# Root columns moved into PSUM and rotation tables moved to GpSimd, in a fused attention and feed-forward kernel on one core

## The chip, the cores and the metric

The kernel runs on one core of a Trainium2 chip. The metric is the time of one execution on the device, in microseconds (us). Engines are named as in the profile: PE is the matrix engine, PEld its weight load, DVE the vector engine, ACT the scalar engine, POOL GpSimd, SP the engine whose queue issues the DMAs. SBUF is the large on-chip buffer, PSUM the smaller one into which PE writes.

## The reference

Everything is float32. A linear attention with its norms comes first, then six layers of the loop below, then a last norm; the change touches the loop alone.

```python
for i in range(6):                       # x is (2, 1024, 128)
    x = attn_layer(shift_tokens(x), Wqkv[i], q_scale[i], k_scale[i], Wo[i]) + x
    x = ffn_layer(shift_tokens(x), ln_g[i], ln_b[i], W1[i], b1[i], W2[i], b2[i]) + x

def attn_layer(x, Wqkv, qs, ksc, Wo):    # 16 heads of 64
    q, k, v = split(x @ Wqkv)
    q = l2norm(q) * qs;  k = l2norm(k) * ksc
    q = q * cos * scale + rotate_half(q) * sin * scale
    k = k * cos / scale + rotate_half(k) * sin / scale
    out = local_attention(q, k, v)       # windows of 32, softmax over 64 keys
    return out @ Wo

def ffn_layer(x, g, bln, W1, b1, W2, b2):
    xn = (x - mean) / sqrt(var + 1e-05) * g + bln
    a, gate = split(xn @ W1 + b1)        # 341 each
    return a * gelu(gate) @ W2 + b2
```

## The kernel before

The 2 x 1024 tokens are 16 blocks of 128. Six layers make 96 blocks, and one step of the main loop works on a pair of them: 48 pairs, `m` = 0 to 47. The loop is software-pipelined. In step `m` the engines project, square and rotate pair `m`, do scores and softmax of pair `m-1`, finish attention, output projection and the centring of the feed-forward norm of pair `m-2`, spread the norm of pair `m-3`, and do the feed-forward matmuls of pair `m-4`. Six steps are unrolled ahead of a loop in registers, four more drain it. Each engine has its own order of instructions, written out by hand in its `step(m)`, and engines meet only by semaphores (`S[...]`, each waited on for a count).

What matters for the change:

- **The rotation tables.** `tables(n, u)` (DVE, L1276) multiplies the rotary table of block `n` (cos, sin for q, cos, sin for k: 4 x 64 columns) by the layer's learned scales into `table[:, u]`, once for each block, at the head of the DVE's step. `turn_cos` (L1287) and `turn_sin` (L1298, two halves) multiply a projection in PSUM by them. POOL adds the two products (`add_q`, `add_k`, L1456).
- **The roots.** `norm_square` (L1304) leaves the sums of squares of 16 heads for q and k of both blocks in `ss` (64 columns). `find_roots(m)`, near the end of the DVE's step, turns them and two columns of variance of the feed-forward norm of pair `m-2` into 67 inverse square roots: L1313 and L1318 write `minus_half`, L1326 forms a first guess on the bits, and three Newton rounds of L1330, L1333 and L1336 follow, each instruction waiting for the one before. All of `minus_half`, `root_t` and `root` are in SBUF.
- **Who waits for the roots.** POOL's `scale_q`, `scale_k` (L1484) multiply the rotated q and k by them: one at the end of its step `m`, three at the head of step `m+1`. PE's `turn_q` and `turn_k` (L786) transpose those. DVE's `residual2(m-4)` (L1386) comes behind `find_roots(m)` in the DVE's order; it raises `x_ready`, for which PE's first `ff_up` (L871) of the next step waits. `ff_down` (L879), the last thing in PE's step, needs a count of `refined` that L1313 and L1318 give.
- **POOL's step** in order: `scale_k`, `scale_q`, `fold_q` (L1469), `scale_k`, `add_q`, `fold_k`, `take_max` (L1495), `add_k`, `take_max`, `fold_q`, `weigh`, `weigh` (L1500), `fold_k`, `add_q`, `add_k`, `scale_q`. The first `weigh` is awaited by PE's `turn_probs(2m-2)` (L786, from `probs`).
- **PE's step** from its middle: both projections at L781, `out_project` (L839) into `pm_out`, projection of k, `turn_probs`, `spread_rstd` (L860), `ff_center` (L846) into `pm_out`, projection of v (which waits for `q_turned`, so for L1298), `ff_var` (L852), `attend` (L830), `ff_down` (L879); then, in the next step, `turn_probs`, projection of q (L781), `ff_up` (L871), `turn_q`, projection of k, `turn_k`, `ff_up` into `pm_out`, and so on.
- **PSUM** is full: `r0`, `r1`, `r2` and `pm`, each two banks. `pm_norm` and `pm_out` are the two banks of `pm`.

Of the kernel before, what the change touches and what calls it, by code (L numbers as in the profile page):

```python
# [19 lines left out]
P = 128  # L20
# [34 lines left out]
def bcast(ap, axis, count):  # L55

    wide = ap.unsqueeze(axis)
    shape = list(wide.shape)
    shape[axis] = count
    return wide.broadcast_to(shape)  # L60
# [566 lines left out]
def layers(nc, weights, xT, ident, mean_w, center_w, eps):  # L627

    with ExitStack() as ctx:
        def sb(name, shape):  # L630
            return ctx.enter_context(nc.sbuf_tensor(name, shape, F32))
# [8 lines left out]
        window, rope, scales = weights.window, weights.rope, weights.scales  # L640


        table = sb("table", [P, 2, 4, DH])
        xs1 = sb("xs1", [P, 2, P])
        squares = sb("squares", [P, 2, INNER])
        ss = sb("ss", [P, QK_ROOTS + 1])
        minus_half = sb("minus_half", [P, ROOTS])
        root_t = sb("root_t", [P, ROOTS])
        root = sb("root", [P, ROOTS])
        warm = sb("warm", [P, 1])  # L650
        warm_exp = sb("warm_exp", [P, 1])
# [21 lines left out]
        hid = sb("hid", [P, 3, W2])  # L673
        r0, r1, r2, pm = psum("r0"), psum("r1"), psum("r2"), psum("pm")
        pm_norm, pm_out = pm[:, 0:512], pm[:, 512:1024]

        names = (
            "v_spread0 v_spread1 "
# [25 lines left out]

            return isinstance(n, int) and n == 0

        def run(eng, step):

            for m in range(FILLED):
                step(m)  # L710
            with eng.Fori(FILLED, PAIRS) as m:
                step(m)
            for m in range(PAIRS, PAIRS + BEHIND):
                step(m)

        def pair_at(m):
# [57 lines left out]
        def _(pe):  # L774
# [108 lines left out]
            def step(m):  # L883
# [78 lines left out]
                if runs(m - 4):  # L962
                    if runs(m - 3):
                        pe.wait_ge(S["xc_squared"], m - 2)
                    elif runs(m - 3):
                        pe.wait_ge(S["residual1"], m - 2)
                    elif runs(m - 5):
                        pe.wait_ge(S["gated"], 3 * (m - 5) + 2)
                    else:
                        pe.wait_ge(S["xc_squared"], m - 3)  # L970
                    ff_up(m - 4, 1, pm_out)
                if runs(m - 1):
                    if runs(m):
# [48 lines left out]
                if runs(m - 2):  # L1022
                    if runs(m - 4):
                        pe.wait_ge(S["gated"], 3 * (m - 4) + 2)
                    elif runs(m - 3):
                        pe.wait_ge(S["xc_squared"], m - 2)
                    elif runs(m - 3):
                        pe.wait_ge(S["residual1"], m - 2)
                    elif runs(m - 5):
                        pe.wait_ge(S["gated"], 3 * (m - 5) + 2)  # L1030
                    elif runs(m - 4):
                        pe.wait_ge(S["xc_squared"], m - 3)
                    elif runs(m - 4):
                        pe.wait_ge(S["residual1"], m - 3)
                    out_project(m - 2)
                if runs(m):
                    if runs(m - 1):
# [233 lines left out]

        @block.vector
        def _(dve):
            def tables(n, u):

                dve.tensor_tensor(table[:, u, :, :].rearrange("p k d -> p (k d)"),  # L1276
                                  rope[:, bass.ds(n % BPB, 1), :, :].rearrange("p a k d -> p (a k d)"),
                                  scales[:, bass.ds(n // NB, 1), :, :].rearrange("p a k d -> p (a k d)"),
                                  ALU.mult).then_inc(S["tabled"], 1)

            def turn_cos(n, u, k, src, squared, turned, transposed):

                dve.wait_ge(S["tabled"], n + 1)
                dve.wait_ge(S[squared], n + 1)
                if not isinstance(n, int) or n >= 2:
                    dve.wait_ge(S[transposed], n - 1)
                dve.tensor_tensor(rot[:, u, k, :, :, :].rearrange("p h a d -> p h (a d)"),  # L1287
                                  src[:, :].rearrange("p (h d) -> p h d", h=HEADS),
                                  bcast(table[:, u, 2 * k, :], 1, HEADS), ALU.mult).then_inc(S[turned], 1)

            def turn_sin(n, u, k, src, turned, added):

                if not first(n):
                    dve.wait_ge(S[added], n)
                v = src[:, :].rearrange("p (h a d) -> p h a d", h=HEADS, a=2)
                for a in range(2):
                    sin = table[:, u, 2 * k + 1, 32 * a:32 * a + 32]
                    dve.tensor_tensor(rot_sin[:, k, :, a, :], v[:, :, 1 - a, :], bcast(sin, 1, HEADS),  # L1298
                                      ALU.mult).then_inc(S[turned], 1)

# [6 lines left out]
            def find_roots(m):  # L1307

                before = ROOT_OPS * m
                if runs(m):  # L1310
                    dve.wait_ge(S["q_summed"], 2 * (m + 1))
                    dve.wait_ge(S["k_summed"], 2 * (m + 1))
                    dve.tensor_scalar(minus_half[:, 0:QK_ROOTS + 1], ss[:, :],  # L1313
                                      1e-24, -0.5, ALU.max, ALU.mult)\
                       .then_inc(S["refined"], 1 if runs(m - LAG) else 2)
                if runs(m - LAG):
                    dve.wait_ge(S["var_done"], m - LAG + 1)
                    dve.tensor_scalar(minus_half[:, QK_ROOTS + 1:ROOTS], pm_norm[:, 0:2], 1e-5, -0.5, ALU.add, ALU.mult)\  # L1318
                       .then_inc(S["refined"], 1 if runs(m) else 2)
                dve.wait_ge(S["refined"], before + 2)  # L1320
                if runs(m - 1):
                    dve.wait_ge(S["q_scaled"], 2 * m)
                    dve.wait_ge(S["k_scaled"], 2 * m)
                if runs(m - LAG - 1):
                    dve.wait_ge(S["rstd_spread"], m - LAG)
                dve.tensor_scalar(root[:, :].bitcast(I32), minus_half[:, :].bitcast(I32), -0.5, GUESS,  # L1326
                                  ALU.mult, ALU.add).then_inc(S["refined"], 1)
                for i in range(NEWTON):
                    dve.wait_ge(S["refined"], before + 3 + 3 * i)
                    dve.tensor_tensor(root_t[:, :], minus_half[:, :], root[:, :], ALU.mult)\  # L1330
                       .then_inc(S["refined"], 1)
                    dve.wait_ge(S["refined"], before + 4 + 3 * i)
                    dve.tensor_tensor(root_t[:, :], root_t[:, :], root[:, :], ALU.mult)\  # L1333
                       .then_inc(S["refined"], 1)
                    dve.wait_ge(S["refined"], before + 5 + 3 * i)
                    dve.scalar_tensor_tensor(out=root[:, :], in0=root_t[:, :], scalar=1.5, in1=root[:, :],  # L1336
                                             op0=ALU.add, op1=ALU.mult).then_inc(S["refined"], 1)
# [52 lines left out]

            def step(m):
                if runs(m):
                    tables(2 * m, 0)
                    tables(2 * m + 1, 1)
                    turn_cos(2 * m, 0, 0, r0, "q_squared", "q_turned", "qT_done")
                    turn_sin(2 * m, 0, 0, r0, "q_turned", "q_added")
                if runs(m - 4):
# [48 lines left out]
        def _(pool):  # L1446
# [46 lines left out]
            def take_max(n, u):  # L1493
                pool.wait_ge(S["maxed"], n + 1)
                pool.tensor_tensor(sm[:, u, :, :], sm[:, u, :, :], bcast(rowmax[:, :], 2, 2 * WIN), ALU.subtract)\  # L1495
                    .then_inc(S["max_taken"], 1)

            def weigh(n, u):
                pool.wait_ge(S["inverted"], n + 1)
                pool.tensor_tensor(probs[:, u, :, :], probs[:, u, :, :], bcast(rinv[:, u, :], 2, 2 * WIN), ALU.mult)\  # L1500
                    .then_inc(S["weighted"], 1)

            def step(m):
                if runs(m - 1):
                    scale_k(2 * m - 2, 0)
                    scale_q(2 * m - 1, 1)
                if runs(m):
                    fold_q(2 * m, 0)
                if runs(m - 1):
                    scale_k(2 * m - 1, 1)  # L1510
                if runs(m):
                    add_q(2 * m, 0)
                    fold_k(2 * m, 0)
                if runs(m - 1):
                    take_max(2 * m - 2, 0)
                if runs(m):
                    add_k(2 * m, 0)
                if runs(m - 1):
                    take_max(2 * m - 1, 1)
                if runs(m):  # L1520
                    fold_q(2 * m + 1, 1)
                if runs(m - 1):
                    weigh(2 * m - 2, 0)
                    weigh(2 * m - 1, 1)
                if runs(m):
                    fold_k(2 * m + 1, 1)
                    add_q(2 * m + 1, 1)
                    add_k(2 * m + 1, 1)
                    scale_q(2 * m, 0)

            run(pool, step)


def last_norm(nc, x1, xT, center_w, eps, out):
# [118 lines left out]
```

## Time and profile before

| | us |
|---|---|
| median of 3 runs | 1858.31 |
| lowest, highest | 1854.05, 1860.98 |
| the profiled execution | 1854.16 |
| its span in the trace | 1852.3 |

| engine | busy us | share of the span |
|---|---|---|
| PE | 1673.8 | 90% |
| DVE | 1562.0 | 84% |
| POOL | 1488.4 | 80% |
| ACT | 1219.1 | 66% |

The linear attention fills roughly the first 120 us; the loop runs from there to about 1838 us. Within it the pattern repeats every 34.2 us, and PE's granted clock is full from 340 us on. A line such as L1484 is a line of the code below, and several operations of one kind can share one. In a timeline row the number in square brackets is how long the engine was idle just before, with what released it.

### The profile page before, as it was taken

How to read it: one execution, taken by the hardware profiler on the slowest of the kernel's cores; microseconds unless marked ns; L12 is line 12 of the kernel's file. 1: busy time of each engine (PE TensorE's matmuls, PEld its weight loads, DVE VectorE, ACT ScalarE, POOL GpSimd, SP SyncE). 2: the span in 40 equal slices, each digit the busy share in tenths (PEclk: the TensorE clock that was granted, in tenths of full speed). 3: DMA queues.
4: the chain of work that ended last, by engine and by line, in shares of the span. 5: the costliest groups of instructions: out<-in, count | busy, mean ns of one | idle time of the engine just before them, and what ended most of it. 6: DMA issues, size and time to landing. Idle time of an engine off the chain costs nothing. (4 is left out here: it accounts for less than half of the span.)

```text
span 1852.3 us, 76505 instructions
## 1 busy us (share of the span) xinstructions
PE 1673.8 (90%) x30992; PEld 1195.4 (65%) x30992; DVE 1562.0 (84%) x2309; ACT 1219.1 (66%) x2072; POOL 1488.4 (80%) x823
## 2 busy tenths in 40 slices
PE   4957889899999999999999999999999999999985
PEld 3634566667667666676676676676666766766664
DVE  6878667898898898988989989988889989899853
ACT  3435455677777767767677777777677676777754
POOL 3568777788888888888888888888888888888851
PEclk7979889999999999999999999999999999999999
DMA  4002132121332221332212232222242223222220
GB/s 136 1 13 57 48 92 60 47 68 45 81 105 75 54 60 48 94 96 68 68 50 67 75 103 55 68 67 66 67 106 59 54 68 79 57 68 68 58 57 23
DMA packets 80697, 121.87 MB, mean 66 GB/s; under 512 B 16776, under 2 KB 29574, under 8 KB 79750
## 3 DMA queue, kind: packets, MB, share of 16 engines
q1 hardware_dynamic: 80646, 121.14, 24.9%
q8 instruction: 38, 0.62, 0.1%
q14 instruction: 13, 0.11, 0.0%
HBM read 19.36 MB, written 1.05 MB: 11 GB/s over the span
## 5 line engine op out<-in xcount | busy, mean ns | idle before, releaser
L781 PE MATMUL r<-wqkv,xs 128*128 (+1 forms) x1152 | 560.7, 618 | 13.4 <-DVE rot_sin L1298 4.3
L1484 POOL TENSOR_TENSOR rot<-rot,root 128x1024 f32<-128x1024 f32 x192 | 377.7, 1987 | 120.6 <-DVE root L1336 120.6
L1456 POOL TENSOR_TENSOR rot<-rot,rot_sin 128x1024 f32<-128x1024 f32 x192 | 451.8, 2364 | 1.6 <-DVE rot_sin L1298 1.6
L781 PEld LDWEIGHTS r<-wqkv,xs 128*128 128x128 f32 x1152 | 210.0, 195 | 213.4 <-issue 197.7
L1131 ACT ACTIVATE squares<-r 128x512 f32<-128x512 f32 x384 | 217.6, 598 | 80.5 <-PE r L781 79.3
L1287 DVE TENSOR_TENSOR rot<-r,table 128x1024 f32<-128x1024 f32 x192 | 232.8, 1213 | 21.0 <-PE r L786 9.6
L1469 POOL TENSOR_TENSOR squares<-squares 128x512 f32<-128x512 f32 x192 | 244.5, 1273 | 6.6 <-ACT squares L1131 6.5
L1500 POOL TENSOR_TENSOR probs<-probs,rinv 128x1024 f32<-128x1024 f32 x96 | 182.7, 1903 | 81.2 <-DVE rinv L1358 81.2
L1298 DVE TENSOR_TENSOR rot_sin<-r,table 128x512 f32<-128x512 f32 x384 | 242.6, 673 | 0.0
L786 PE MATMUL r<-square,rot 128*128 128x128 f32 x1536 | 208.4, 279 | 17.3 <-POOL rot L1484 11.8
L786 PEld LDWEIGHTS r<-square,rot 128*128 128x128 f32 x1536 | 169.5, 141 | 81.2 <-issue 27.5
L1495 POOL TENSOR_TENSOR sm<-sm,rowmax 128x1024 f32<-128x1024 f32 x96 | 182.6, 1902 | 45.4 <-DVE rowmax L1350 45.1
L1343 DVE TENSOR_TENSOR sm<-r,window 128x1024 f32<-128x1024 f32 x96 | 117.6, 1225 | 109.6 <-PE r L814 109.6
L1166 ACT ACTIVATE qT<-r 128x1024 f32<-128x1024 f32 x96 | 98.2, 1023 | 165.6 <-PE r L786 165.6
L871 PE MATMUL pm<-xn,w 128*128 128x256 f32 (+1 forms) x576 | 153.4, 390 | 58.4 <-DVE xT L1386 57.8
L830 PE MATMUL r<-pT,vwin 64*64 64x32 f32 x12288 | 202.9, 221 | 2.6 <-issue 2.6
L830 PEld LDWEIGHTS r<-pT,vwin 64*64 64x64 f32 x12288 | 191.7, 137 | 13.5 <-issue 12.9
L839 PE MATMUL pm<-attnT,wo 128*128 128x256 f32 x768 | 175.5, 382 | 1.2 <-issue 1.2
L839 PEld LDWEIGHTS pm<-attnT,wo 128*128 128x128 f32 x768 | 147.0, 192 | 41.2 <-issue 23.3
L1276 DVE TENSOR_TENSOR table<-rope,scales 128x256 f32 (+1 forms) x96 | 155.5, 1658 | 10.2 <-issue 10.1
L871 PEld LDWEIGHTS pm<-xn,w 128*128 128x128 f32 (+1 forms) x576 | 93.9, 180 | 107.7 <-issue 87.0
L1116 ACT ACTIVATE kT<-r 128x1024 f32<-128x1024 f32 x96 | 98.3, 1024 | 96.6 <-PE r L786 91.4
(123 smaller groups left out, 2723.2 us busy)
## 6 DMA issues: line engine op xcount, KB each, us to landing
vwin<-vtok SPq DMA_DIRECT2D x576, 128.0 KB, 2.3
vwin<-vtok SPq DMA_DIRECT2D x384, 64.0 KB, 2.0
wqkv<-in_wqkv SPq DMA_DIRECT2D x6, 1536.0 KB, 8.3
wo<-in_wo SPq DMA_DIRECT2D x6, 512.0 KB, 4.9
w<-in_w SPq DMA_DIRECT2D x6, 341.0 KB, 2.9
x<-in_x SPq DMA_DIRECT2D x4, 256.0 KB, 3.6
rope<-in_rope SPq DMA_DIRECT2D x1, 1024.0 KB
out_x<-y SPq DMA_DIRECT2D x4, 256.0 KB, 2.3
```

The lines of the kernel that those rows point to most:

```text
L781: pe.matmul(dst[:, c * 512:(c + 1) * 512], xs1[:, u, :], w.rearrange("p a n -> p (a n)"), start=True, stop=True).then_inc(S[done], 1)
L786: last = pe.transpose(dst[:, f * P:(f + 1) * P], src[:, f * P:(f + 1) * P], ident)
L830: last = pe.matmul(dst[DH * s:DH * (s + 1), at + WIN * w:at + WIN * (w + 1)], vwin[half, u, w, 2 * i + s, :], pT[half, u, (FT // 2) * s + ...
L839: last = pe.matmul(pm_out[:, 0:W2], wo[:, f, :], attnT[:, (f % 2) * (FT // 2) + f // 2, :], start=(f == 0), stop=(f == FT - 1))
L871: last = pe.matmul(dst[0:rows, half * W2:(half + 1) * W2], w1[:, half * FF + at:half * FF + at + rows], xn2[:, :], start=True, stop=True)
L1131: last = act.activation(squares[:, k, c * 512:(c + 1) * 512], src[:, c * 512:(c + 1) * 512], ACT.Square)
L1287: dve.tensor_tensor(rot[:, u, k, :, :, :].rearrange("p h a d -> p h (a d)"), src[:, :].rearrange("p (h d) -> p h d", h=HEADS), bcast(table ...
L1298: dve.tensor_tensor(rot_sin[:, k, :, a, :], v[:, :, 1 - a, :], bcast(sin, 1, HEADS), ALU.mult).then_inc(S[turned], 1)
L1456: pool.tensor_tensor(r, r, rot_sin[:, k, :, :, :].rearrange("p h a d -> p h (a d)"), ALU.add)\
L1469: pool.tensor_tensor(halves[:, :, 0, :], halves[:, :, 0, :], halves[:, :, 1, :], ALU.add)\
L1484: pool.tensor_tensor(r, r, bcast(root[:, at:at + HEADS], 2, DH), ALU.mult)\
L1500: pool.tensor_tensor(probs[:, u, :, :], probs[:, u, :, :], bcast(rinv[:, u, :], 2, 2 * WIN), ALU.mult)\
```

## The change

- `minus_half` and `root_t` are no longer SBUF tensors but the first 134 columns of `pm_out`. `root` stays in SBUF. L1313 now comes behind the wait for the variance and runs in every step, since other contents of the bank destroy its columns in between; PE waits for all of the roots of the step before ahead of `ff_up` into `pm_out` and of `out_project`.
- The tables are multiplied on POOL, one instruction for both blocks of a pair (512 columns), a step ahead, between the second `fold_q` and the first `weigh`. `table` has two buffers. DVE's `turn_cos` and `turn_sin` address theirs by a register.

```diff
-        table = sb("table", [P, 2, 4, DH])
+        table = sb("table", [P, 2, 2, 4, DH])
...
-        minus_half = sb("minus_half", [P, ROOTS])
-        root_t = sb("root_t", [P, ROOTS])
...
+        minus_half, root_t = pm_out[:, 0:ROOTS], pm_out[:, ROOTS:2 * ROOTS]
...
+                    pe.wait_ge(S["refined"], ROOT_OPS * (min(m, PAIRS + LAG) if isinstance(m, int) else m))
                     ff_up(m - 4, 1, pm_out)
...
+                    pe.wait_ge(S["refined"], ROOT_OPS * (min(m, PAIRS + LAG) if isinstance(m, int) else m))
                     out_project(m - 2)
...
-            def tables(n, u):
-
-                dve.tensor_tensor(table[:, u, :, :].rearrange("p k d -> p (k d)"),
-                                  rope[:, bass.ds(n % BPB, 1), :, :].rearrange("p a k d -> p (a k d)"),
-                                  scales[:, bass.ds(n // NB, 1), :, :].rearrange("p a k d -> p (a k d)"),
-                                  ALU.mult).then_inc(S["tabled"], 1)
-
             def turn_cos(n, u, k, src, squared, turned, transposed):
 
-                dve.wait_ge(S["tabled"], n + 1)
+                dve.wait_ge(S["tabled"], n // 2 + 1)
...
-                                  bcast(table[:, u, 2 * k, :], 1, HEADS), ALU.mult).then_inc(S[turned], 1)
+                                  bcast(table[:, bass.ds((n // 2) % 2, 1), u, 2 * k, :].rearrange("p a d -> p (a d)"),
+                                        1, HEADS), ALU.mult).then_inc(S[turned], 1)
...
-                    sin = table[:, u, 2 * k + 1, 32 * a:32 * a + 32]
+                    sin = table[:, bass.ds((n // 2) % 2, 1), u, 2 * k + 1, 32 * a:32 * a + 32]\
+                        .rearrange("p a d -> p (a d)")
...
                 if runs(m):
                     dve.wait_ge(S["q_summed"], 2 * (m + 1))
                     dve.wait_ge(S["k_summed"], 2 * (m + 1))
-                    dve.tensor_scalar(minus_half[:, 0:QK_ROOTS + 1], ss[:, :],
-                                      1e-24, -0.5, ALU.max, ALU.mult)\
-                       .then_inc(S["refined"], 1 if runs(m - LAG) else 2)
                 if runs(m - LAG):
                     dve.wait_ge(S["var_done"], m - LAG + 1)
+                dve.tensor_scalar(minus_half[:, 0:QK_ROOTS + 1], ss[:, :],
+                                  1e-24, -0.5, ALU.max, ALU.mult)\
+                   .then_inc(S["refined"], 1 if runs(m - LAG) else 2)
+                if runs(m - LAG):
                     dve.tensor_scalar(minus_half[:, QK_ROOTS + 1:ROOTS], pm_norm[:, 0:2], 1e-5, -0.5, ALU.add, ALU.mult)\
-                       .then_inc(S["refined"], 1 if runs(m) else 2)
+                       .then_inc(S["refined"], 1)
...
             def step(m):
                 if runs(m):
-                    tables(2 * m, 0)
-                    tables(2 * m + 1, 1)
...
+            def tables(m):
+
+                if not isinstance(m, int) or m >= 2:
+                    pool.wait_ge(S["q_turned"], 6 * (m - 1))
+                    pool.wait_ge(S["k_turned"], 6 * (m - 1))
+                pool.tensor_tensor(table[:, bass.ds(m % 2, 1), :, :, :].rearrange("p a u k d -> p (a u) (k d)"),
+                                   rope[:, bass.ds((m % PPB) * 2, 2), :, :].rearrange("p a k d -> p a (k d)"),
+                                   bcast(scales[:, bass.ds(m // PPL, 1), :, :].rearrange("p a k d -> p (a k d)"), 1, 2),
+                                   ALU.mult).then_inc(S["tabled"], 1)
...
                 if runs(m):
                     fold_q(2 * m + 1, 1)
+                if runs(m + 1):
+                    tables(m + 1)
                 if runs(m - 1):
                     weigh(2 * m - 2, 0)
...
-            run(pool, step)
+            pool.wait_ge(S["tables_loaded"], 7 * 16)
+            tables(0)
+            run(pool, step, PAIRS - 1)
```

## Rows read from the trace of the kernel before

**Rows 1.** The page: busy time, share of the span and instructions of each engine.
```profile
PE 1673.8 (90%) x30992; PEld 1195.4 (65%) x30992; DVE 1562.0 (84%) x2309; ACT 1219.1 (66%) x2072; POOL 1488.4 (80%) x823
```

**Rows 2.** Busy time in the steady stretch: PE, PEld, DVE, ACT, POOL, clock, DMA.
```profile
340.00:1800.00 1460.00, 1377.53 (x26812) 996.94 (x26811) 1287.04 (x1859) 1025.84 (x1692) 1253.77 (x678) 1.00 0.27 69
```

**Rows 3.** Groups of PE, same stretch: busy us, mean ns, idle before and releaser.
```profile
L871 PE MATMUL pm<-xn,w 128*128 128x256 f32 x340 | 91.5, 392 | 53.9 <-DVE xT L1386 53.9
...
L879 PE MATMUL pm<-hid,w 128*128 128x256 f32 x168 | 47.3, 404 | 12.2 <-DVE minus_half L1318 12.2
```

**Rows 4.** Timeline of PE over the end of one step and the next one's head.
```profile
1047.62 1.04 PE L786 MATMUL r<-square,probs 128*128 128x128 f32 x8
...
1048.93 0.60 PE L846 MATMUL pm<-xs,center_w 128*128 128x256 f32 x2
1049.62 1.98 PE L781 MATMUL r<-wqkv,xs 128*128 x4
1051.43 0.50 PE L852 MATMUL pm<-square,xcsq 128*128 128x1 f32 x4
1051.86 2.07 PE L830 MATMUL r<-pT,vwin 64*64 64x32 f32 x128
1054.23 1.56 PE L879 MATMUL pm<-hid,w 128*128 128x256 f32 x6 [0.30 <-DVE minus_half L1318]
...
1056.50 1.88 PE L781 MATMUL r<-wqkv,xs 128*128 x4
1059.63 1.13 PE L871 MATMUL pm<-xn,w 128*128 128x256 f32 x4 [1.25 <-DVE xT L1386]
```

**Rows 5.** Timeline of DVE, same stretch, and one row a pair earlier.
```profile
1019.83 2.21 DVE L1326 TENSOR_SCALAR root<-minus_half 128x67 int32<-128x67 int32 x1
...
1052.83 1.10 DVE L1313 TENSOR_SCALAR minus_half<-ss 128x65 f32<-128x65 f32 x1
1053.86 0.15 DVE L1318 TENSOR_SCALAR minus_half<-pm 128x2 f32<-128x2 f32 x1
1054.04 2.22 DVE L1326 TENSOR_SCALAR root<-minus_half 128x67 int32<-128x67 int32 x1
1056.29 0.23 DVE L1330 TENSOR_TENSOR root_t<-minus_half,root 128x67 f32<-128x67 f32 x1
...
1058.39 0.23 DVE L1336 SCALAR_TENSOR_TENSOR root<-root_t,root 128x67 f32<-128x67 f32 x1
1058.86 0.48 DVE L1386 SCALAR_TENSOR_TENSOR xT<-pm,cols,mid 128x256 f32 x1 [0.24 <-issue]
1059.58 3.34 DVE L1276 TENSOR_TENSOR table<-rope,scales 128x256 f32 x2 [0.24 <-issue]
```

**Rows 6.** Timeline of POOL over the same stretch.
```profile
1041.64 1.90 POOL L1495 TENSOR_TENSOR sm<-sm,rowmax 128x1024 f32<-128x1024 f32 x1
1043.50 1.28 POOL L1469 TENSOR_TENSOR squares<-squares 128x512 f32<-128x512 f32 x1
1044.74 1.90 POOL L1500 TENSOR_TENSOR probs<-probs,rinv 128x1024 f32<-128x1024 f32 x1
1048.42 1.90 POOL L1500 TENSOR_TENSOR probs<-probs,rinv 128x1024 f32<-128x1024 f32 x1 [1.78 <-DVE rinv L1358]
...
1051.51 4.69 POOL L1456 TENSOR_TENSOR rot<-rot,rot_sin 128x1024 f32<-128x1024 f32 x2
1058.70 5.99 POOL L1484 TENSOR_TENSOR rot<-rot,root 128x1024 f32<-128x1024 f32 x3 [2.50 <-DVE root L1336]
```

**Rows 7.** Three lines of DVE, each alone: duration in ns, min/median/max.
```profile
L1326 DVE TENSOR_SCALAR root<-minus_half x50: 195/2212/2287, 141.4 to 1820.5; 128x67 int32<-128x67 int32 x50
...
L1276 DVE TENSOR_TENSOR table<-rope,scales x96: 416/2015/2123, 119.8 to 1743.7; 128x256 f32 x84, 128x256 f32<-128x256 f32 x12
...
L1371 DVE TENSOR_TENSOR xhat<-xc,pm x48: 408/411/422, 249.0 to 1829.6; 128x256 f32<-128x256 f32 x48
L1371 DVEq FUSED_REGOPS  x42: 125/127/127, 366.7 to 1766.4; - x42
```

More of the change, by code:

```diff
@@ L705, in first, with run @@
             return isinstance(n, int) and n == 0
-        def run(eng, step):
+        def run(eng, step, end=PAIRS):
             for m in range(FILLED):
                 step(m)
-            with eng.Fori(FILLED, PAIRS) as m:
+            with eng.Fori(FILLED, end) as m:
                 step(m)
-            for m in range(PAIRS, PAIRS + BEHIND):
+            for m in range(end, PAIRS + BEHIND):
                 step(m)
```

## The prediction

> **What bounds the kernel now.** I read the page first: no engine is full, PE comes nearest, then DVE and POOL [rows 1]. The busy times of the steady stretch say how much room there is. L1326 comes at 1019.83 and again at 1054.04 [rows 5], so a pair takes 34.2 us, and 1460 us are 42.7 pairs. PE is idle 1460 - 1377.5 = 82.5 us there, 1.93 us in each pair, so a pair can't take less than 34.2 - 1.93 = 32.3 us by PE's work. DVE needs 30.1 us in each pair, POOL 29.4 [rows 2]. So PE is the bound but for its small idle times, and the question of every part of the change is what it does to these.
>
> The groups of PE then say whose they are: 53.9 us in front of `ff_up` behind DVE's `xT` and 12.2 us in front of `ff_down` behind DVE's `minus_half`, 66.1 of the 82.5 us [rows 3]. In the timeline of one step they are 1.25 and 0.30 us [rows 4].
>
> The DVE's timeline beside POOL's shows why `xT` is late. L1313 starts at 1052.83 and takes 1.10 us for 65 columns; L1326 starts at 1054.04 and takes 2.22 us for 67, while the Newton instructions of the same width take 0.23 [rows 5]. POOL runs two `add` from 1051.51 to 1056.20, so about 2.35 us each: the first ends near 1053.9, the second at 1056.20. L1313 ends at 1053.93, L1326 at 1056.26 [rows 5, 6]. Each ends just after a POOL instruction does. L1326 can take 195 ns and has a median of 2212; the tables' L1276 can take 416 ns and has a median of 2015 [rows 7]. These work SBUF to SBUF. L1318, which reads PSUM, starts in between and takes 0.15 us though the second `add` has begun [rows 5, 6]; L1371, one input in PSUM and one in SBUF, never takes more than 422 ns [rows 7]. I read this as: a DVE instruction that works on SBUF alone waits for the POOL instruction in progress, one with an operand in PSUM does not.
>
> **The roots' columns in PSUM.** L1313 then writes PSUM and L1326 reads it. Without the waits they cost what the Newton instructions do, 0.23 us: 1.10 + 2.22 - 0.46 = 2.86 us less for each pair [rows 5]. The last L1336 ends at 1058.62 now, so at 1055.76 then; `xT` ends at 56.48 instead of 59.34 [rows 5] (the leading 10 is left off from here). L1313's new place behind `var_done` costs nothing: `ff_var` ends at 51.93, DVE comes there at 52.83 [rows 4, 5].
>
> What follows on PE: L1318 ends near 53.2, before `attend` ends at 53.93, so `ff_down` starts at 53.93 and not at 54.23. The projection then ends at 58.08, `xT` is there since 56.48 (PE started 0.29 us after its end before, so 56.77), and `ff_up` starts at once [rows 4, 5]. Both PE stalls go, 66.1 / 42.7 = 1.55 us for each pair. What is late next is `turn_q`: POOL is free at 56.20, later than the roots, and its first `scale` takes 1.90, to 58.10 (1.90 is what L1495 takes at the same width, and what a scale takes once DVE's tables don't hold it up); PE comes there at 58.08 + 1.03 = 59.1 [rows 4, 6]. That is 1.0 us of cover. The two `pe.wait_ge` on `refined` come long after the roots and cost nothing.
>
> The trace has no DVE instruction that writes PSUM. From below, the price is nothing: L1318 takes 0.15 us for two columns, the Newton instructions 0.23 for 67, which are 0.08 apart for 65 columns more [rows 5]. From above, I take a doubled pace of the nine Newton instructions and L1326, 0.26 us each (L1330 starts at 56.29, the ninth at 58.39, 0.263 apart [rows 5]): 2.6 us more. The cover is 0.44 us (roots at 55.76, POOL free at 56.20) and 1.0 us at `turn_q`, 1.4 together, so it decides from 0.14 us for each of ten instructions; the upper end would give back 1.2 us a pair. I take the lower end, since the nearest rows read PSUM without a surcharge.
>
> The Trainium skill speaks against that: its page "VectorE: DVE Perf Modes", section on the TRN2 errata, gives 120 fixed cycles for an instruction from PSUM and 58 from SBUF. At 0.96 GHz that is 65 ns more, an estimate of 0.65 us for the ten. By it the roots would come at 56.41, POOL's scale would end 0.2 us later, and the sum would be the same. The trace doesn't bear the rule out for reads: two columns from PSUM took 146 ns in all.
>
> **The tables off DVE.** Two L1276 take 3.34 us, directly behind `xT` and ahead of `turn_cos` [rows 5]. Nobody on PE waits for `turn_cos` in that place, so this is DVE idle time gained, not path. It has one more effect: three scales take 5.99 us for 3 x 1.90, 0.29 us of POOL's time lost to the tables in between [rows 6]. DVE falls to 30.1 - 3.3 - 2.9 = 23.9 us a pair and can't bind by amount.
>
> **The tables on POOL.** A POOL instruction on 512 columns from two inputs takes 1.28 us (L1469), on 1024 columns 4.69 / 2 = 2.35 (L1456), and one whose second input repeats 1.90 for 1024 (L1500) [rows 6]. So it is (2.35 - 1.28) / 512 = 2.09 ns a column and 0.21 us fixed, and with a repeating input (1.90 - 0.21) / 1024 = 1.65 ns, which gives 1.06 us for 512. Between 1.06 and 1.28 I take 1.28, of which 1.24 show up in the pace (43.50 to 44.74). Its register arithmetic is hidden under the running `fold` as L1371's 127 ns are, or exposed with the 0.24 us of the DVE's tables [rows 5, 7]; I take half, 0.12.
>
> The place is the first `weigh`: it starts at 44.74 and then at 44.74 + 1.24 + 0.12 = 46.10, and ends at 48.00 instead of 46.64. PE starts `turn_probs` at 47.62 [rows 4, 6]. Everything ahead of it on POOL is tied to PE (`take_max` follows the scores), so this doesn't shift away: PE stalls 0.38 us. Of it 0.09 is swallowed: PE waits from 49.53 to 49.62 in front of the projection of v for DVE's `turn_sin`, which isn't delayed [rows 4]. Net 0.29 us a pair. The second `weigh` has 1.78 us of idle time ahead of it and isn't moved [rows 6]. The bounds: 1.06 and nothing exposed costs 0 (`weigh` ends at 47.7, and 0.09 is swallowed); 1.24 and 0.24 cost 0.41.
>
> The DVE's twelve turns of a pair now have register addresses. L1371's shows as 127 ns under a running instruction with no idle time of its own [rows 7]; I take nothing. If exposed, the place is the two `turn_sin` ahead of PE's projection of v, which are on PE's heels: 2 x 0.24 = 0.5 us a pair.
>
> **The sum.** The stalls go in the 44 steps that have both (m = 4 to 47): 44 x 1.55 = 68.2 us. The table's stall comes in 47: 47 x 0.29 = 13.6 us. Net -54.6. The span goes from 1852.3 to 1797.7, a profiled execution from 1854.16 to about 1799.6. The median of the runs shown is 1858.31, 4 us above the profiled one, and I expect the same of the new kernel: 1858.3 - 54.6 = 1803.7, so **1804 us**. By the bounds of the table alone it is 1790 to 1809.
>
> **The rivals.**
>
> *The forecast*, both stalls go and a small one comes, 1790 to 1815 us: 0.56. A pair takes about 32.9 us.
>
> *More given back*: Newton in PSUM is slower than 0.14 us an instruction above today's, or `turn_sin`'s addresses are exposed. The first at its upper end gives back 1.2 us x 44 = 53 us, 1857 (the chance of that far end is small); the second 0.5 x 47 = 23 us, 1827. Between them, 1815 to 1848: 0.20. For it speaks that no row shows a PSUM write; against it, L1318 and L1371.
>
> *More gained*: the table's stall is hidden, and the 0.38 us a pair of PE's idle time that is neither stall shrinks with DVE freed. At most 44 x 1.93 = 85 us, 1773; I put 1775 to 1790 at 0.12.
>
> *POOL becomes the bound.* It would have 29.4 - 0.3 + 1.3 = 30.4 us of work in a pair of 32.9. It binds by amount only if the table took over 3.8 us, three times the nearest row; part of the 0.06 at 1850 to 1867, no change.
>
> *The other side: PSUM doesn't free DVE from POOL.* Then L1313 and L1326 end with POOL's instructions as before, `xT` ends at 59.34, both stalls stay, and only the table's 0.29 us x 47 = 14 us is new: 1872. It decides only if L1326 still waits: if L1313 alone did, the roots would come 0.9 us later than forecast, at 56.6, and nearly all of the gain would stay, but if L1326 alone did, none of the 1.25. L1318 and L1371 speak against it. Chance 0.06.
>
> **The numbers.** A measurement of this kernel can tell about 0.5% (9 us) from no change. Faster 0.56 + 0.20 + 0.12 = 0.88; within 0.5%, 0.06; slower 0.06. The range 1784 to 1840 holds the forecast, half of the further gain and most of what is given back, and leaves out about 0.2.
>
> **What would show it.** In the new profile: L1313 and L1326 at 0.2 to 0.3 us; no idle time in front of L871 behind `xT` nor of L879 behind `minus_half`; POOL's scale without its 2.50 us wait for `root`; a POOL instruction of 1.05 to 1.3 us for the table; a new wait of PE's `turn_probs` for `probs` near 0.3 us; DVE idle while it waits for ACT's squares. The prediction is wrong if L1326 still takes 2 us, if the Newton pace is above 0.40 us, or if PE has a new stall above 1 us in a pair.

## The result: 0.943 of the time before, twice the gain that was forecast

The changed kernel takes 1751.18 us (median of 4 runs, 1747.19 to 1756.07) against 1856.18 for the kernel before on the same chips. The ratio is 0.9434, 95% interval 0.9394 to 0.9473: 105 us less. The forecast was 1804 us (54.6 less), with a range of 1784 to 1840. The sign was right and the mechanism did what it should, but the gain was nearly twice its size and the time lies below the range.

The page of the changed kernel, its busy times (its span is 1745.4 us):

```profile
PE 1638.7 (94%) x30992; PEld 1203.5 (69%) x30992; DVE 1279.3 (73%) x2215; ACT 1219.8 (70%) x2072; POOL 1528.9 (88%) x871
```

The busy times of its steady stretch, columns as in [rows 2]:

```profile
340.00:1700.00 1360.00, 1340.91 (x26548) 1003.05 (x26547) 1030.93 (x1779) 1023.76 (x1686) 1276.27 (x712) 1.00 0.28 74
```

A pair is measured here from one `residual1` to the next. In the kernel before, 38 of them lie between 431.9 and 1695.3 us: 1263.4 / 37 = 34.15 us. In the changed one, 41 lie between 408.4 and 1688.4: 1280 / 40 = 32.00 us. From the first of the 48 to the last it is 1612.8 us before and 1506.9 after, 105.9 of the 106.9 us by which the spans differ. So the whole gain is in the loop, 2.15 us in each pair of the steady part; 1.26 was forecast (1.55 - 0.29). The first four distances between them give more: 203.9 to 363.7 us before, 200.8 to 344.4 after, 16.2 us less and not 4 x 2.15 = 8.6. PE's granted clock isn't full there in either kernel (200 to 270 and 270 to 340 us: 0.88 and 0.95 before, 0.93 and 0.98 after), and in the kernel before it is still 0.97 from 340 to 400 us, so "full from 340 us on" was a little too early.

The DVE's timeline at the roots shows the wait for POOL gone, as forecast. These rows answer to [rows 5]:

```profile
1022.18 0.23 DVE L1313 TENSOR_SCALAR pm<-ss 128x65 f32<-128x65 f32 x1
1022.32 0.16 DVE L1317 TENSOR_SCALAR pm<-pm 128x2 f32<-128x2 f32 x1
1022.51 0.23 DVE L1325 TENSOR_SCALAR root<-pm 128x67 int32<-128x67 int32 x1
1022.77 0.24 DVE L1329 TENSOR_TENSOR pm<-pm,root 128x67 f32<-128x67 f32 x1
...
1024.92 0.23 DVE L1335 SCALAR_TENSOR_TENSOR root<-pm,root 128x67 f32<-128x67 f32 x1
1025.38 0.48 DVE L1385 SCALAR_TENSOR_TENSOR xT<-pm,cols,mid 128x256 f32 x1 [0.23 <-issue]
```

1.10 and 2.22 us have become 0.23 and 0.23. It is so in every step: 48 of the 50 L1325 start while a POOL instruction runs, and none takes more than 229 ns. In the kernel before, 47 of the 50 L1326 took about 2.2 us, and each of these ended 0.05 to 0.06 us after a POOL instruction did; the three short ones (under 0.3 us) started when POOL was idle. The Newton chain moves at (1024.92 - 1022.77) / 8 = 0.269 us against 0.263 in SBUF. DVE then waits 3.52 us, for PE's transposes (L786) and not for ACT's squares as the prediction had it.

POOL, which answers to [rows 6]:

```profile
1014.03 1.29 POOL L1500 TENSOR_TENSOR table<-rope,scales  x1
1015.27 1.91 POOL L1507 TENSOR_TENSOR probs<-probs,rinv 128x1024 f32<-128x1024 f32 x1
1017.72 1.90 POOL L1507 TENSOR_TENSOR probs<-probs,rinv 128x1024 f32<-128x1024 f32 x1 [0.54 <-DVE rinv L1357]
...
1020.80 4.69 POOL L1453 TENSOR_TENSOR rot<-rot,rot_sin 128x1024 f32<-128x1024 f32 x2
1025.43 5.64 POOL L1481 TENSOR_TENSOR rot<-rot,root 128x1024 f32<-128x1024 f32 x3
```

The table takes 1.29 us (1.28 was taken), with nothing exposed for its registers; the scales follow the adds without the 2.50 us wait, and three of them take 5.64 us, not 5.99. The 1.78 us ahead of the second `weigh` are 0.54.

PE, in the same place of the step as [rows 4]:

```profile
1015.20 1.88 PE L781 MATMUL r<-wqkv,xs 128*128 x4
1017.33 1.06 PE L786 MATMUL r<-square,probs 128*128 128x128 f32 x8 [0.25 <-POOL probs L1507]
...
1018.67 0.60 PE L846 MATMUL pm<-xs,center_w 128*128 128x256 f32 x2
1019.11 1.88 PE L781 MATMUL r<-wqkv,xs 128*128 x4
1020.82 0.50 PE L852 MATMUL pm<-square,xcsq 128*128 128x1 f32 x4
1021.26 2.07 PE L830 MATMUL r<-pT,vwin 64*64 64x32 f32 x128
1023.25 1.56 PE L879 MATMUL pm<-hid,w 128*128 128x256 f32 x6
...
1025.53 1.88 PE L781 MATMUL r<-wqkv,xs 128*128 x4
1027.25 1.03 PE L871 MATMUL pm<-xn,w 128*128 128x256 f32 x4
1028.11 1.04 PE L786 MATMUL r<-square,rot 128*128 128x128 f32 x8
1028.99 1.88 PE L781 MATMUL r<-wqkv,xs 128*128 x4
```

Both old stalls are gone and the new one at `turn_probs` is there. The rows also show how the size was misread. Look at the starts alone. The projection at 1025.53 is "busy" for 1.88 us, yet the next group starts 1.72 us after it: where PE is never held up, a group starts before the modelled end of the one ahead, 0.16 us before it behind a projection and 0.07 behind `attend` (2.07 busy, 2.00 from start to start). An idle entry counts from that end, so it is short by that much for each stall, and a short wait leaves a gap too small for an entry, or none.

More rows of the kernel before. First, the projection of k, which nothing holds up, and the groups behind the stalled `ff_up`:

```profile
1045.90 1.88 PE L781 MATMUL r<-wqkv,xs 128*128 x4
...
1060.65 1.09 PE L786 MATMUL r<-square,rot 128*128 128x128 f32 x8
1061.59 1.88 PE L781 MATMUL r<-wqkv,xs 128*128 x4
```

The next show a wait without an entry. They are PE at its second `ff_up` and second `turn_q`, its weight load there, and DVE just ahead:

```profile
1029.96 1.03 PE L871 MATMUL pm<-xn,w 128*128 128x256 f32 x4
1031.09 1.09 PE L786 MATMUL r<-square,rot 128*128 128x128 f32 x8
1032.02 1.03 PE L871 MATMUL pm<-xn,w 128*85 128x256 f32 x4
```

```profile
1031.09 0.86 PEld L786 LDWEIGHTS r<-square,rot 128*128 128x128 f32 x8 [0.50 <-DVE rot_sin L1298]
```

```profile
1029.76 1.27 DVE L1298 TENSOR_TENSOR rot_sin<-r,table 128x512 f32<-128x512 f32 x2
```

DVE's `turn_sin` ends at 1031.03, and PE's `turn_q` into the same `r0` starts at 1031.09. From `ff_up` to it are 1.13 us. PE's own gap is 0.10 us and not listed, but the weight load names the wait: 20.2 us behind `rot_sin` in 40 of these from 340 to 1700 us, and in the changed kernel none. There the same place takes 0.86:

```profile
1031.58 1.03 PE L871 MATMUL pm<-xn,w 128*128 128x256 f32 x4
1032.44 1.04 PE L786 MATMUL r<-square,rot 128*128 128x128 f32 x8
1033.32 1.03 PE L871 MATMUL pm<-xn,w 128*85 128x256 f32 x4
```

The differences of one pair, from start to start on PE:

| place | before | after | gained | forecast |
|---|---|---|---|---|
| `attend` to `ff_down` | 2.37 | 1.99 | 0.38 | 0.30 |
| projection of q to `ff_up` | 3.13 | 1.72 | 1.41 | 1.25 |
| `ff_up` to `turn_q`, and to the projection of k | 1.02 + 0.94 | 0.86 + 0.88 | 0.22 | 0 |
| second `ff_up` to second `turn_q`, and on | 1.13 + 0.93 | 0.86 + 0.88 | 0.32 | 0 |
| `ff_center` to projection of v, and on | 0.69 + 1.81 | 0.44 + 1.71 | 0.35 | 0.09 |
| projection of k to `turn_probs` | 1.72 | 2.13 | -0.41 | -0.38 |

They sum to 2.27 us; the mean over the stretch is 2.15. The pair shown is typical: over all whole steps from 340 to 1700 us (39 before, 41 after) the mean at each of these places is within 0.02 us of the table. With 0.03 lost behind `turn_probs` and 0.02 at the scores, these means add up to 2.18, which is what PE's step itself shrinks by.

### The profile page after: what moved, and what is told of

It reads as the page before. It is cut to its first block and busy times, and to the rows that moved or that the text cites. A ratio compares the mean times of both kernels' runs of the same rounds, so it can differ in the third digit from the quotient of the medians.

```text
span 1745.4 us, 77175 instructions
## 1 busy us (share of the span) xinstructions
PE 1638.7 (94%) x30992; PEld 1203.5 (69%) x30992; DVE 1279.3 (73%) x2215; ACT 1219.8 (70%) x2072; POOL 1528.9 (88%) x871
## 5 line engine op out<-in xcount | busy, mean ns | idle before, releaser
L781 PE MATMUL r<-wqkv,xs 128*128 (+1 forms) x1152 | 551.8, 609 | 10.8 <-DVE rot_sin L1295 5.1
L1481 POOL TENSOR_TENSOR rot<-rot,root 128x1024 f32<-128x1024 f32 x192 | 361.2, 1902 | 1.0 <-DVE root L1335 1.0
L786 PEld LDWEIGHTS r<-square,rot 128*128 128x128 f32 x1536 | 175.7, 141 | 44.4 <-ACT qT L1168 15.2
L786 PE MATMUL r<-square,rot 128*128 128x128 f32 x1536 | 202.3, 275 | 2.4 <-POOL rot L1481 1.1
L1118 ACT ACTIVATE kT<-r 128x1024 f32<-128x1024 f32 x96 | 98.3, 1024 | 95.9 <-PE r L786 90.3
L814 PE MATMUL r<-kT,qT 64*32 64x64 f32 x12288 | 146.7, 226 | 17.0 <-issue 16.8
L814 PEld LDWEIGHTS r<-kT,qT 64*32 64x32 f32 x12288 | 129.6, 105 | 37.9 <-issue 36.0
```

Source lines behind the costliest of these rows:

```text
L781: pe.matmul(dst[:, c * 512:(c + 1) * 512], xs1[:, u, :], w.rearrange("p a n -> p (a n)"), start=True, stop=True).then_inc(S[done], 1)
L786: last = pe.transpose(dst[:, f * P:(f + 1) * P], src[:, f * P:(f + 1) * P], ident)
L814: last = pe.matmul(dst[rows, at:at + 2 * WIN], qT[half, u, f, rows], kT[half, u, f, WIN * w:WIN * (w + 2)], start=True, stop=True)
L1481: pool.tensor_tensor(r, r, bcast(root[:, at:at + HEADS], 2, DH), ALU.mult)\
```

## The experiments

All ratios are to the kernel before on the same chip. **Theory S**: PE's loss by a stall is what the starts show, more than the idle entry, and the roots' part carries the gain. Its rivals are in each expectation.

### Each part alone

Roots' columns in PSUM, tables left on DVE. Against the changed kernel (`tables(n, u)` and the table's buffer are as in the kernel before, too):

```diff
                 if runs(m):
+                    tables(2 * m, 0)
+                    tables(2 * m + 1, 1)
                     turn_cos(2 * m, 0, 0, r0, "q_squared", "q_turned", "qT_done")
...
                 if runs(m):
                     fold_q(2 * m + 1, 1)
-                if runs(m + 1):
-                    tables(m + 1)
```

> Roots' columns in PSUM, tables as before on DVE. Theory S (PE's loss from a stall is larger than the idle entry in front of it, because back-to-back groups start before the modelled end of the one before; the loss is read from start to start): this part alone removes 0.38 us at ff_down, 1.41 at ff_up and 0.22 behind it in each pair, and up to 0.3 more at the second turn_q, so a pair takes 31.9 to 32.2 us against 34.2 and the ratio to before is 0.940 to 0.950. Rival T (the gain beyond the forecast came from the tables leaving DVE): this part gives its forecast 68 us alone, ratio near 0.963, a pair near 32.6 us.

Measured: 1744.9 us, ratio 0.9397 (0.9371 to 0.9422); a pair 31.93 us. The pair lies in what Theory S expected and the ratio a hair under its 0.940, and rival T is out: this part alone gives 113 us, more than its forecast 68. Its PE at the projection of v:

```profile
1014.99 1.88 PE L781 MATMUL r<-wqkv,xs 128*128 x4
1016.70 1.04 PE L786 MATMUL r<-square,probs 128*128 128x128 f32 x8
...
1018.02 0.60 PE L846 MATMUL pm<-xs,center_w 128*128 128x256 f32 x2
1018.70 1.98 PE L781 MATMUL r<-wqkv,xs 128*128 x4
1020.52 0.50 PE L852 MATMUL pm<-square,xcsq 128*128 128x1 f32 x4
```

`turn_probs` is not held up (1.71), but the old waits at the projection of v stand (0.68 and 1.82). The second `turn_q` is free here too, although DVE still does the tables.

Tables on POOL, roots' columns in SBUF, one line away from the changed kernel:

```diff
-        minus_half, root_t = pm_out[:, 0:ROOTS], pm_out[:, ROOTS:2 * ROOTS]
+        minus_half, root_t = sb("minus_half", [P, ROOTS]), sb("root_t", [P, ROOTS])
```

> Tables on POOL, the roots' columns in SBUF. Theory S: both big stalls of PE stay, a stall of 0.4 us at turn_probs comes in the place of 0.35 us at the projection of v, and 0.3 us at the second turn_q goes: ratio 0.988 to 1.003. Rival T: the tables' part carries what the forecast missed, about 40 to 50 us, ratio 0.973 to 0.980. L1325 keeps its 2.2 us in both.

Measured: 1845.48 us, ratio 0.9932 (0.9915 to 0.9949); a pair 33.84 us. As Theory S has it. L1313 keeps its new place behind the wait for the variance here, and L1325 its 2210 ns (median), so what frees DVE is PSUM and not the order: this one line is worth 33.84 - 32.00 = 1.84 us a pair. PE's stall in front of `ff_up` is untouched:

```profile
1018.23 1.88 PE L781 MATMUL r<-wqkv,xs 128*128 x4
1021.36 1.13 PE L871 MATMUL pm<-xn,w 128*128 128x256 f32 x4 [1.25 <-DVE xT L1385]
```

The parts alone give 2.22 and 0.31 us a pair, 2.53 together, and 2.15 when both are there. They don't add up, since two waits are shortened by either: the second `turn_q` (0.32), and 0.09 of the one at `ff_down`. 2.53 - 0.41 = 2.12. With the roots in PSUM, the tables' part gives 0.35 us at the projection of v and takes 0.45 at and behind `turn_probs` (means over all steps).

### One column set in SBUF

```diff
-        minus_half, root_t = pm_out[:, 0:ROOTS], pm_out[:, ROOTS:2 * ROOTS]
+        minus_half, root_t = pm_out[:, 0:ROOTS], sb("root_t", [P, ROOTS])
```

> As the changed kernel, but root_t in SBUF, so that the second instruction of each Newton round has both inputs in SBUF. If a DVE tensor_tensor with two SBUF inputs waits for POOL as well, the first L1332 takes about 2.4 us (until POOL's second add ends) instead of 0.24, xT comes 2.2 us later, PE stalls about 1.2 us in front of ff_up, and the ratio is 0.970 to 0.976. If only the instructions with one SBUF input and an SBUF output wait, L1332 stays at 0.23 us and the ratio is that of the change, 0.943.

Measured: 1812.95 us, ratio 0.9753 (0.9736 to 0.977); a pair 33.08 us. The time is as expected, and the wait came back, but at L1335, one instruction later than expected. DVE, then POOL:

```profile
1028.28 0.23 DVE L1329 TENSOR_TENSOR root_t<-pm,root 128x67 f32<-128x67 f32 x1
1028.55 0.23 DVE L1332 TENSOR_TENSOR root_t<-root_t,root 128x67 f32<-128x67 f32 x1
1028.81 2.28 DVE L1335 SCALAR_TENSOR_TENSOR root<-root_t,root 128x67 f32<-128x67 f32 x1
```

```profile
1026.32 4.69 POOL L1453 TENSOR_TENSOR rot<-rot,rot_sin 128x1024 f32<-128x1024 f32 x2
```

POOL's second add ends at 1031.01 and L1335, with both inputs in SBUF, at 1031.09. L1329, with one input in PSUM, runs beside the first add. L1332 waits as well, for the first add, but it comes so late that this costs nothing: it starts 0.144 us before that add's end, near 1028.69, and takes 0.229. In other steps it came earlier: 0.21 us before the end it took 0.298, 0.53 before it 0.62, and 2.25 before it 2.342, its longest. Each time it ended 0.09 us after that add, also where the next add followed directly, as here. The wait for the second add then fell to L1335. So the `tensor_scalar` of L1313 and L1325 and the two-input instructions wait if all their tensors are in SBUF, and one operand in PSUM frees them. Not every instruction on SBUF alone waits: of the reductions over `probs` (L1355 in the changed kernel) 89 of 96 start while POOL runs, and the longest takes 1220 ns, the mean 1209. The prediction's reading was too wide there. The Trainium skill states the second case, in "SBUF — State Buffer", section "Who interferes with whom": two SBUF inputs contend with a GpSimd instruction that reads SBUF. The trace agrees, with 2.28 us for L1335.

### A delay of known size

Two reductions on DVE, unused, between the roots and `xT`:

```diff
+                    for i in range(2):
+                        dve.tensor_reduce(idle_out[:, i, :], bcast(window[:, :, :].rearrange("p a k -> p (a k)"), 1, 4), AX.X, ALU.max)
                     residual2(m - 4)
```

> As the changed kernel, with two DVE reductions over 1024 columns each (about 2.3 us together) between the roots and xT in every step. xT then ends about 28.1 where the changed kernel has it at 25.86, PE starts ff_up about 1.05 us later than at 27.25, and the idle entry in front of it should be about 0.85. Theory S: a pair grows by 1.05 and the restart behind it, 0.2, so 1.25 us, more than the idle entry says: 44 x 1.25 = 55 us, ratio 0.972. Rival I (the idle entry is the loss, and PE's shorter busy time in the changed kernel has another cause): 44 x 0.85 = 37 us, ratio 0.963, and the groups behind ff_up keep the shorter times.

Measured: 1803.7 us, ratio 0.9709 (0.9683 to 0.9735); a pair 32.99 us. PE:

```profile
1020.34 1.88 PE L782 MATMUL r<-wqkv,xs 128*128 x4
1023.01 1.13 PE L872 MATMUL pm<-xn,w 128*128 128x256 f32 x4 [0.79 <-DVE xT L1386]
1023.97 1.04 PE L787 MATMUL r<-square,rot 128*128 128x128 f32 x8
```

The idle entry is 0.79 us (32.1 us for 41 pairs), the pair grew by 0.99. From start to start the projection takes 2.67 instead of 1.72 (0.95 more) and `ff_up` 0.96 instead of 0.86. That is the misreading on its own: a stall costs more than its entry, by 0.2 us if read from the pair and by 0.26 at the place itself. Both theories missed the size: 1.25 us a pair was expected by Theory S and 0.85 by its rival. The restart was over-expected (0.2; it is 0.1 here), and only the direction, above the entry, speaks for S. The ratio (0.972 expected) fits in part by luck: between this trace and the changed kernel's, 3.2 of the 55.5 us are there before the first delay runs, and 7.2 come in the drain behind the last whole step. The time of a pair is the clean reading.

### The table's place

```diff
                 if runs(m - 1):
                     weigh(2 * m - 2, 0)
+                if runs(m + 1):
+                    tables(m + 1)
+                if runs(m - 1):
                     weigh(2 * m - 1, 1)
```

> As the changed kernel, but POOL's tables between the two weigh instead of ahead of them. The second weigh has 0.54 us of idle time ahead and the first is free of 1.24 us, so the stall at turn_probs goes. PE then reaches the projection of v 0.4 us earlier and meets DVE's turn_sin there, which would give up to 0.35 us back: ratio 0.934 to 0.943. If the stall at turn_probs is no loss at all, the ratio stays 0.943; if all of it is gained, 0.933.

Measured: 1741.7 us, ratio 0.9382 (0.9359 to 0.9405); a pair 31.91 us. The stall at `turn_probs` is gone (1.72 from start to start), and 0.71 and 1.82 us are back at the projection of v. Net 0.09 us a pair against the changed kernel, 4 us. Of the 7.0 us by which the spans differ, 3.7 come between the `residual1` near 405 us and the one near 1685, and 2.5 ahead of the first. Once more, with more executions:

> The version with the tables between the two weigh once more, on the same chip as the others of this set: 31.9 us a pair, ratio 0.936 to 0.942.

Measured: 1746.44 us, ratio 0.9399 (0.9375 to 0.9424).

> The version with the roots' part alone once more, on the same chip as the others of this set: 31.9 us a pair, ratio 0.937 to 0.943, no slower than the whole change. So the tables' part gives nothing where it is placed in the change.

Measured: 1749.54 us, ratio 0.9398 (0.9372 to 0.9423), a pair 31.9 us. And the change itself once more, against runs of the kernel before of its own:

> The changed kernel itself, on the same chip as the others of this set: ratio 0.941 to 0.946.

Measured: 1748.93 us, ratio 0.9433 (0.9407 to 0.946), a pair 31.97. The change as made is no faster than its roots' part alone; if anything 0.35% slower, but the intervals overlap. The traces point the same way, 32.00 and 31.97 us a pair against 31.93 and 31.90.

### The next wait, and the next

DVE is idle 0.78 us ahead of `residual1`, and PE waits for `turn_sin` two instructions later. Moved ahead:

```diff
                     norm_square(2 * m + 1, 1, 0, "q_folded", "q_summed")
+                    turn_sin(2 * m + 1, 1, 0, r1, "q_turned", "q_added")
                 if runs(m - 2):
                     residual1(m - 2)
...
                 if runs(m):
-                    turn_sin(2 * m + 1, 1, 0, r1, "q_turned", "q_added")
                     turn_cos(2 * m + 1, 1, 1, r0, "k_squared", "k_turned", "kT_done")
```

> Changed kernel with the tables between the two weigh, and DVE's turn_sin for q of the second block moved ahead of residual1, where DVE is idle 0.78 us. Theory S: PE's start-to-start from ff_center to the projection of v falls from 0.7 to 0.44 and the projection from 1.82 to 1.71, so 0.35 us a pair less than with the tables alone moved, ratio 0.929 to 0.932 (about 1.0 to 1.4% under the changed kernel). If residual1, which comes 0.45 us later, delays ff_center instead, no gain: 0.938.

Measured: 1751.04 us, ratio 0.9434 (0.9414 to 0.9454), a pair 31.89 us. Outside both expectations: no gain, and in time 9 us more than without this edit (0.9434 against 0.9382; with the second measurement, 0.9399, the interval overlaps by a little), though a pair is no longer: the `residual1` that comes at 405.0 us there comes at 413.7 here, with a granted clock of 0.95 from 270 to 400 us against 1.00. `ff_center` wasn't late; the wait went one group further, to `ff_var`, which waits for DVE's `xhat`:

```profile
1022.80 1.88 PE L781 MATMUL r<-wqkv,xs 128*128 x4
1024.81 0.61 PE L852 MATMUL pm<-square,xcsq 128*128 128x1 f32 x4
```

The same `turn_sin` moved in the version with the roots' part alone:

> Root columns in PSUM, tables left on DVE, and the same turn_sin moved ahead of residual1. If the place of the tables is worth nothing by itself once turn_probs isn't held up, this is as fast as the version with the tables between the weigh: ratio 0.929 to 0.933. If the tables on DVE cost PE through POOL's three scales (0.3 us) or the second turn_q, it is 0.934 to 0.940.

Measured: 1753.74 us, ratio 0.9447 (0.9428 to 0.9466), a pair 32.0 us. That misses both expectations too and is slower than the roots' part alone (0.9397): the wait for `xhat` is there (1.91 us from start to start in the mean), and 0.16 us are back at the second `turn_q`, where the weight load waits for `rot_sin` again (13.9 us in 41). Then, with the tables between the two `weigh` again, `ff_norm`, which makes `xhat`, ahead of the `turn_cos` of k too:

```diff
+                if runs(m - 3):
+                    ff_norm(m - 3)
                 if runs(m):
                     turn_cos(2 * m + 1, 1, 1, r0, "k_squared", "k_turned", "kT_done")
-                if runs(m - 3):
-                    ff_norm(m - 3)
```

> As the version with the tables between the weigh and turn_sin moved ahead of residual1, and ff_norm moved ahead of the turn_cos of k, since there ff_var waited for xhat (start to start of the projection of v 2.01 instead of 1.72). If that was the only thing late next, a pair takes 31.55 to 31.65 us instead of 31.9, and the ratio is 0.928 to 0.933. If the wait moves on once more (to x-hat's own wait for rstd_spread, or to POOL), a pair stays at 31.9 and the ratio at 0.937 to 0.943.

Measured: 1744.46 us, ratio 0.9377 (0.9357 to 0.9397), a pair 31.76 us. PE:

```profile
1018.57 0.60 PE L846 MATMUL pm<-xs,center_w 128*128 128x256 f32 x2
1019.00 1.88 PE L781 MATMUL r<-wqkv,xs 128*128 x4
1020.82 0.58 PE L852 MATMUL pm<-square,xcsq 128*128 128x1 f32 x4
```

0.43 and 1.82 us instead of 0.71 and 1.82, but `ff_var` takes longer to its successor (0.51, 0.43 where nothing holds it). Over all steps, the loss at these three groups falls from 0.38 to 0.19 us: half of the wait is gone, between the two expectations. It is the shortest pair of all, though in time it can't be told from the version with only the tables moved (0.9399).

## Why the prediction was wrong

**The mechanism was right, three sizes were not.** L1313 and L1325 at 0.23 us each, `xT` early, both stalls of PE gone, POOL's wait for the roots gone, the table at 1.29 us: each as forecast, and the experiment with `root_t` in SBUF shows that it is the operand in PSUM that frees DVE. Neither part alone is a loss.

**The step that failed is the size of the stalls**: "Both PE stalls go, 66.1 / 42.7 = 1.55 us for each pair." The idle entries were taken for the loss. By the starts the same two places gave 0.38 + 1.41, and 0.22 in the groups behind, 2.01 us. With 2.01 in its place the prediction's own sum would have come to about 1784, the edge of the range; the next two terms took it past that. The rows to see it were there: in [rows 4] the projection at 1056.50 is busy until 1058.38, while the working of the change let `ff_up` start at 58.08 after moving that group up by only 0.30, so a start to start of 1.88 was assumed where 1.72 is what PE does when nothing holds it (the group of the same size that starts at 1045.90 is followed at 1047.62). The delay experiment measured the difference by itself: 0.79 shown, 0.99 lost. The difference isn't one number: over all steps, gap and loss are 1.25 and 1.62 at `ff_up`, 0.29 and 0.36 at `ff_down`, 0.26 and 0.45 at the new stall of `turn_probs`.

**"A pair can't take less than 32.3 us by PE's work"** fell with it. It added up modelled busy times, and these are longer behind a stall (`ff_up` 1.13 us against 1.03, the projection of v 1.98 against 1.88). The changed kernel's pair takes 32.00 us, the last version's 31.76; PE's busy time itself fell from 1377.5 / 42.7 = 32.3 to 1340.9 / 42.5 = 31.6 us a pair.

**"Nobody on PE waits for `turn_cos` in that place, so this is DVE idle time gained, not path"** was wrong too, worth 0.32 us a pair: the second `turn_q` waited for `turn_sin` behind DVE's tables. No PE idle entry names it; DVE's end at 1031.03 against PE's start at 1031.09 does, and so does the weight load's wait. Either part alone removes it.

**The swallowed wait** in front of the projection of v was taken at 0.09 and is 0.35 (0.25 and 0.10 by the starts). The table's stall was taken at 0.38 and is 0.41, 0.44 with the group behind. So the table's stall costs little net, 0.1 us a pair, where 0.29 was charged. Moving the table confirmed it: 0.09 us a pair.

**The sum again**: 2.01 + 0.32 + 0.35 - 0.44 (0.03 of it at `spread_rstd`) = 2.24 us in this pair against 1.26 forecast. Of the 0.98 between them, the size of the two stalls is 0.46, the second `turn_q` 0.32, the swallowed wait 0.26, and the table -0.06. Times 44 it is 99 us. What is left to 106.9 is about the 7.6 us by which the first four distances shrink more than the steady ones, for which the forecast had no term.

**The PSUM price** at its lower end was right: Newton instructions went from 228 to 236 ns where they read and write PSUM, the pace from 0.263 to 0.269 us, 0.05 us for the chain. The 65 ns an instruction that the prediction estimated from the Trainium skill's page "VectorE: DVE Perf Modes", section on the TRN2 errata, are not there: the third Newton instruction takes 228 ns with all inputs in SBUF (L1336) and 228 with one in PSUM (L1335). The 146 ns of two columns that the prediction set against the Trainium skill's page could not decide this, since they are more than 120 cycles at 0.96 GHz. The other rivals did not come: next to nothing was given back by the register addresses of `turn_sin` (two take 1.25 us, 1.22 before), POOL did not become the bound, and the far side (DVE not freed) was excluded by the first row of the new trace.

What stays open: how much of the differences of some microseconds in the first 400 us between nearly equal kernels is the granted clock there; why the groups behind a stall are further apart (by 0.10 to 0.22 us behind `ff_up`); and whether 0.9434 against 0.9398 for the roots' part alone is a difference.

## What to carry to other kernels

Read the loss of a stall on a nearly full matrix engine from start to start, against the same group where nothing holds it up, and look there also where no idle entry stands, and at the waits of the weight load; idle entries were a lower bound in each case here. A small chain of vector instructions on the critical path is worth an operand in PSUM when GpSimd is busy beside it: two instructions of 0.23 us were costing 3.3. And when two edits free the same wait, time each alone, since the second may bring nothing.

## What the runs showed of the hardware

- A `tensor_scalar` or two-input DVE instruction of 65 or 67 columns, all in SBUF, takes up to 2.3 us beside POOL instructions and ends 0.05 to 0.09 us after one of them does; with one operand in PSUM it takes 0.23 to 0.24 us. Reductions on SBUF alone don't wait (1220 ns at most for 1024 columns).
- POOL instructions that follow one another directly still let a waiting DVE instruction in between them. One that starts 0.14 us before the end of the running POOL instruction loses nothing (0.229 us at 1028.55 in the half-PSUM version), one that starts 2.25 us before it takes 2.342.
- An instruction of 67 columns that reads PSUM takes DVE 8 ns more when it writes PSUM than when it writes SBUF (236 against 228, L1329 in the changed and in the half-PSUM version).
- A stall of PE costs more than the gap in its records: 0.07 us more behind `attend`, 0.19 at `turn_probs`, 0.26 at the delayed `ff_up` and 0.37 at the old one.
